# Fill products and new orders of begin and end in a kernel of four conditioned residual layers

## The chip, the cores and the metric

One core of a Trainium2 chip. The metric is the time of one execution on the device, in microseconds (us), of this core. Each kernel is run several times; the median counts. The profile is of one execution of its own: its span runs from the first to the last instruction, and some time lies around it.

## The reference

Inputs are x, 128 entries of 64 rows of 256 numbers, and per entry a vector of 128, one of 64 and one of 32. Four layers follow, each added to its input:

```python
x = x + L0(x)   # U = mu @ W_dec + b_dec, (257, 30) per entry; weight = U @ V; out = x @ weight + bias
x = x + L1(x)   # styles = mu @ affine.T; (x * styles) @ weight.T * dcoefs + bias, clipped to +-256
x = x + L2(x)   # relu(x @ (down * dg + db)) @ (up * ug + ub) + x, gains and offsets from mu
x = x + L3(x)   # below
# L3: h = ln(ln(x, pw[id]), cp[id]); t = ln(x, tm[id]); s = ln(x, ms[id])
#     m, n, r = x + mlp_ln(memory), x + mlp_ln(noise), x + mlp_ln(resource)
#     out = mlp_ln(concat(w0 h, w1 t, w2 m, w3 n, w4 r, w5 s)), w = softmax(aw)
```

Here `mlp_ln` is two matrix products with a silu between them and a layer norm behind. What hangs on the entry alone (U, styles, dcoefs, the gains of L2, the three small nets) is computed once ahead of the blocks.

## The kernel before, in words

The 8192 rows are cut into 16 blocks of 512 (8 entries each). A block goes through some sixty stages on four engines. TensorE (PE) has 17 stages per block, ScalarE (ACT) 17, VectorE (DVE) 19, GpSimd (POOL) 9; SyncE (SP) issues the loads and stores. Stages of one engine run in an order that is written out by hand: `run_slots` (L81) goes through the list `begin`, then ten times through `order` (the loop, for all blocks in turn: a pair (stage, lag) runs for the block that many behind), then through `end`. A pair (stage, n) in `begin` and `end` is that stage for block n. Each engine runs its list strictly in order; a stage waits on semaphores for what it reads and for the tiles that it overwrites.

The data of a block: `pe_t` and `pe_x1` (L0, L919, L935) give x1; POOL's `g_style` (L1516) makes xm; `pe_l1` (L948) and DVE's `v_l1mul`, `v_l1min`, `v_x2add` (L1352, L1361, L1367) make x2; `pe_dn` (L962), `v_dnmul`, `v_dnadd`, `act_relu`, and `pe_up` (L976) make x3. The weights of `pe_up` are made by POOL's `g_wup` (two products of tensors, L1565 and L1567) from a tile `ugub` that is loaded per block. `pe_x3r` (L988) turns x3, `v_xstat` takes the statistics, `g_rootx` (L1523 to L1531) the inverse root, `act_xnorm` (L1209) xhat; `g_gather` (L1507) fetches four tiles of table rows by indirect DMAs, `g_hmul` and `g_hadd` (L1546, L1551) make h, `v_hstat`, `g_rooth`, `act_hnorm`, `v_hprod` finish it. `g_res` (L1577) makes x3be, which only the last step of a block reads. `pe_xht`, `pe_hht` (L994) are transposes, `pe_tm` (L1008), `pe_ms`, `pe_cp` look up gains by onehot products, `pe_shift` (L1074) and `pe_w1_x3`, `pe_w1_tm`, `pe_w1_ms`, `pe_w1_h` (L902 to L904) sum the first product of the last MLP, `pe_w2` (L1132 and L902 to L904) is the second; `act_ysquare`, `v_ygain`, `g_rooty`, `v_ynorm` are the last layer norm. In the last three blocks (`fine`) the silu and the second product are cut in halves.

Ahead of the blocks stands the setup. The decoder: `load_dec` brings W_dec, 16 groups of up to four matrices are copied into another order by `act_turn` (L696, 11 groups) and `v_turn` (L587, 5 groups), multiplied by `pe_dec` (L487) and taken from PSUM by `v_decode` (L595) into six banks used in turn. W_dec's place in memory is used again: `load_w2n`, `load_w1` and `load_rown` (L456, L465, L460) wait for the last product of the decoder (`m_dec` of 16). Three nets run through `pe_hid`, `act_hid`, `pe_mo`, `v_mostat`, `g_moroot`, `v_monorm`, `pe_mot`, `act_mot`, `pe_row`; `pe_cls` and `v_classes` make the class rows. `act_ubwrite` (L701) issues three writes of the bias rows, `act_ug` (L727, L729) writes the table that `load_up` reads. `v_dcrcp` and `g_dcoef` make dcoefs, which `v_l1mul` 0 waits for. `g_w2low`, `g_w1xlow`, `g_w1tlow`, `g_w1mlow` (L832 to L846) make the low halves of the last MLP's weights.

`pe_warm` (L531 to L537) runs products of a tile of ones that nobody reads, into a PSUM bank that is free at the time. In the kernel before it has four places with 13, 13, 7 and 13 products; each place waits for one semaphore, given in its table, and for five of POOL's memsets. The tile of ones is set in `g_init` (L796), behind seven DMA issues of POOL.

## Time and profile before

| | us |
|---|---|
| three runs | 521.61, 525.68, 526.17 |
| median | 525.68 |
| profiled execution | 521.21 |
| its span | 519.4 |
| one block of the loop on PE | 27.8 |
| first block of the loop starts on PE | 96.7 |

The rows are read so: in a timeline, the first number is the start in us, the second how long the instruction or the merged group (xcount) took, then engine, line, operation, the tile written and the tiles read. What stands in brackets is the idle time of the engine ahead of it and what ended it. PE's weight loads are a row of their own (PEld). One f32 product is two records.

### The profile page before, as it was taken

The page shows a single profiled execution, that of the slowest core. Times are in us where ns is not written, and L with a number is a line of the kernel's source. Part 1 is how long each engine was busy: PE and PEld are TensorE (multiplying, and loading weights), DVE is VectorE, ACT ScalarE, POOL GpSimd, SP SyncE. Part 2 cuts the span into 40 slices and gives each one's busy share as a digit, 9 for nine tenths or more (in the row PEclk, how much of TensorE's full clock was granted, in tenths as well). Part 3 has the DMA queues.
Part 4 walks back from the last instruction along what each step waited for, and adds up shares of the span by engine and source line. Part 5 has one row for each costly group of instructions (what it writes and reads, how often), then busy time and mean ns, then how long its engine had stood idle before and what let it go on. Part 6 is the DMA issues. An engine that isn't in the chain of part 4 may idle for free.

```text
span 519.4 us, 9425 instructions
## 1 busy us (share of the span) xinstructions
PE 486.3 (94%) x3198; PEld 354.2 (68%) x3198; DVE 405.8 (78%) x696; ACT 336.3 (65%) x638; POOL 391.0 (75%) x367
## 2 busy tenths in 40 slices
PE   2987887999999999999999999999999999998993
PEld 2953644767677776768686867677776768687682
DVE  2958876868788788888787878788787888886863
ACT  4573667456767676766777776767676767656832
POOL 6468799889878879697978787788779793787321
PEclk9999999999999999999999999999999999999997
DMA  8887705625252352608080716253442613104102
GB/s 299 247 304 208 203 20 124 163 73 135 83 127 81 77 171 56 191 24 223 0 229 17 205 43 173 74 136 112 106 142 63 175 47 90 49 21 145 40 2 81
DMA packets 34989, 61.78 MB, mean 119 GB/s; under 512 B 5017, under 2 KB 17413, under 8 KB 34580
## 3 DMA queue, kind: packets, MB, share of 16 engines
q1 hardware_dynamic: 28756, 43.98, 30.2%
q0 software_dynamic: 5344, 16.87, 11.3%
q10 hardware_dynamic: 864, 0.61, 0.4%
q8 instruction: 14, 0.23, 0.2%
q14 instruction: 11, 0.09, 0.1%
HBM read 52.58 MB, written 8.87 MB: 118 GB/s over the span
## 4 chain that ended last, share of the span: by engine, by line
PE 79%; POOL 6%; DVE 5%; DMA 4%; issue 3%; ACT 2%; SPq 0%; DVEq 0%; POOLq 0%; ACTq 0%
PE ps_c L902 11%; PE ps_c L904 11%; PE ps_c L903 10%; PE ps_d L948 9%; PE ps_d L962 5%; PE ps_a L976 5%; PE ps_b L902 3%; PE ps_b L903 3%; PE ps_b L904 3%; PE ps_b L935 2%; PE ps_a L988 2%; DMA set_wdec<-in_nets_rows 2%; PE ps_a L994 2%; PE ps_b L994 2%; DMA set_wdec<-in_W_dec 1%
## 5 line engine op out<-in xcount | busy, mean ns | idle before, releaser
L1507 POOL DMA_INDIRECT pw_rows<-in_pw,gidx x64 | 65.0, 1016 | 17.9 <-issue 17.4
L948 PE MATMUL ps_d<-xm_t,l_w 128*128 128x512 f32 x128 | 59.0, 603 | 2.2 <-POOL xm_t L1516 2.2
L1209 ACT ACTIVATE h<-h,nb_h,rstd_h 128x256 f32<-128x256 f32 x64 | 33.3, 591 | 33.1 <-POOL nb_h L1531 33.0
L1240 ACT ACTIVATE tm_t_h<-ps_a 128x1024 fp32r<-128x1024 f32 x16 | 16.4, 1026 | 45.6 <-DVE ps_a L1413 45.6
L1516 POOL TENSOR_TENSOR xm_t<-x_t,style 128x1024 f32<-128x1024 f32 x16 | 30.5, 1905 | 20.2 <-DVE x_t L1345 20.1
L948 PEld LDWEIGHTS ps_d<-xm_t,l_w 128*128 128x128 f32 x128 | 23.1, 190 | 26.8 <-issue 24.2
L1546 POOL TENSOR_TENSOR h<-xhat,pw_rows 128x1024 f32<-128x1024 f32 x16 | 38.0, 2378 | 4.1 <-ACT xhat L1209 4.1
L1565 POOL TENSOR_TENSOR w_up<-up_rep,ugub 128x1024 f32<-128x1024 f32 x16 | 38.0, 2372 | 2.2 <-issue 2.0
L1551 POOL TENSOR_TENSOR h<-h,pw_rows 128x1024 f32<-128x1024 f32 x16 | 38.3, 2394 | 1.3
L1567 POOL TENSOR_TENSOR w_up<-w_up,ugub 128x1024 f32<-128x1024 f32 x16 | 38.1, 2382 | 1.3
L902 PE MATMUL ps_b<-w_h,act_t_l 128*128 128x256 f32 x128 | 37.7, 294 | 0.4 <-DVE act_t_l L1450 0.4
L1577 POOL TENSOR_TENSOR x3be<-x,ln_gb 128x1024 f32<-128x1024 f32 x16 | 37.8, 2364 | 0.0
L1352 DVE TENSOR_TENSOR ps_d<-ps_d,dcoef 128x1024 f32<-128x1024 f32 x16 | 19.7, 1232 | 21.6 <-PE ps_d L948 21.6
L903 PE MATMUL ps_b<-w_l,act_t_h 128*128 128x256 f32 x128 | 36.1, 282 | 0.0
L904 PE MATMUL ps_b<-w_h,act_t_h 128*128 128x256 f32 x128 | 36.0, 281 | 0.0
L1209 ACT ACTIVATE xhat<-ps_a,nb_x,rstd_x 128x256 f32<-128x256 f32 x64 | 31.0, 564 | 6.7 <-POOL nb_x L1531 6.7
L962 PE MATMUL ps_d<-x_t,down_w 128*64 128x256 f32 x256 | 31.2, 385 | 3.0 <-DVE x_t L1367 3.0
L976 PEld LDWEIGHTS ps_a<-act_dn,w_up 128*128 128x128 f32 x256 | 30.5, 191 | 4.9 <-issue 2.6
L976 PE MATMUL ps_a<-act_dn,w_up 128*128 128x128 f32 x256 | 31.6, 277 | 2.2 <-ACT act_dn L1188 1.2
L1590 POOL TENSOR_TENSOR ve_y<-y_var,eps 128x4 f32<-128x4 f32 x15 | 3.0, 202 | 40.2 <-ACT y_sq L1320 40.2
L1418 DVE TENSOR_TENSOR ps_d<-ps_d,xh_t 128x1024 f32<-128x1024 f32 x16 | 19.7, 1231 | 17.4 <-PE ps_d L1031 17.4
L1320 ACT ACTIVATE y_sq<-ps_b 128x256 bf16<-128x256 f32 x64 | 23.7, 380 | 14.8 <-PE ps_b L904 14.8
(251 smaller groups left out, 1551.2 us busy)
## 6 DMA issues: line engine op xcount, KB each, us to landing
ugub<-ugub_scratch SPq DMA_DIRECT2D x32, 512.0 KB, 6.8
x_t<-in_x_t SPq DMA_DIRECT2D x16, 512.0 KB, 5.7
out<-y_out SPq DMA_DIRECT2D x15, 512.0 KB, 7.3
set_wdec<-in_W_dec SPq DMA_DIRECT2D x2, 1920.0 KB, 9.6
set_wdec<-in_int_W SPq DMA_DIRECT2D x1, 1536.0 KB, 9.8
set_wdec<-in_nets_rows SPq DMA_DIRECT2D x1, 1152.0 KB, 12.2
pw_rows<-in_pw,gidx POOLq DMA_INDIRECT x64, 3.7
set_wdec<-in_nets_W SPq DMA_DIRECT2D x1, 768.0 KB, 4.8
```

Source lines behind the costliest of these rows:

```text
L902: eng.matmul(out, wl, ah, start=first, stop=False)
L903: eng.matmul(out, wh, al, start=False, stop=False)
L904: return eng.matmul(out, wh, ah, start=False, stop=last)
L948: m = eng.matmul(ps_l1[:, o, :], l1_w[:, k, o * P:(o + 1) * P], xm_t[:, k, :], start=k == 0, stop=k == KB - 1)
L962: m = eng.matmul(ps_dn[e * HID:(e + 1) * HID, part * CT * S:(part + 1) * CT * S], down_w[:, k, part * HID:(part + 1) * HID], x[:, k, e], s ...
L976: m = eng.matmul(ps_up[:, k, j * P:(j + 1) * P], w_up[:, j, k * P:(k + 1) * P], act_dn[:, j, :, :], start=True, stop=True)
L1209: m = eng.activation(out[:, j, :], src[:, j, :], ACT.Identity, bias=nb[k][:, j:j + 1], scale=rstd[k][:, j:j + 1])
L1507: eng.indirect_dma_start(pw_rows[c.ring][:, j, :], None, t["pw"], bass.IndirectOffsetOnAxis(ap=gidx[c.ring][:, j:j + 1], axis=0)).then_inc ...
L1546: eng.tensor_tensor(h1[:, :, :], xhat[:, :, :], pw_rows[c.ring][:, :, 0:D], ALU.mult).then_inc(g_h1m, 1)
L1551: eng.tensor_tensor(h1[:, :, :], h1[:, :, :], pw_rows[c.ring][:, :, D:2 * D], ALU.add).then_inc(g_h1, 1)
L1565: eng.tensor_tensor(w_up[:, :, :], q, ugub[:, :, 0:D], ALU.mult).then_inc(g_upm, 1)
L1567: eng.tensor_tensor(w_up[:, :, :], w_up[:, :, :], ugub[:, :, D:2 * D], ALU.add).then_inc(g_up, 1)
```

## The change

The loop's orders and SP's list are unchanged. POOL sets the tile of ones first of all (`g_ones`), and `pe_warm` waits for that alone. It has seven places in its table `WARM` (semaphore, value, bank, half, count): 27 products ahead of the decoder, 6 ahead of `pe_mo`, 23 ahead of `pe_dn` 0, 12 ahead of `pe_dn` 1, 4 behind it, 9 ahead of `pe_t` 3 and 11 ahead of `pe_hht` 0. That is 92 products where 46 were. `begin` and `end` of all four engines get new orders. The stages themselves and their durations are the same. The lists of ScalarE, VectorE and POOL are shown as they are after the change; those of before stand above.

```diff
@@ -409,6 +409,9 @@
         pads = (ubias_p[:, :], act_dn[:, :, :, :], onehot[0][:, :], onehot[1][:, :], shift[0][:, :], shift[1][:, :], gain_tab[:, 2 * D:3 * D],)
 
 
+        WARM = ((z_pool, 1, ps_b, 0, 27), (c_ug, 1, ps_d, 0, 6), (v_dca, 1, ps_a, 0, 23), (v_x1, 2, ps_b, 0, 4),
+                (v_row, 1, ps_c, 0, 12), (v_cls, 1, ps_c, 1, 9), (v_row, 1, ps_c, 0, 11))
+
         def load_front(eng, c):
             eng.dma_start(mu, t["cond_side"][:, 0:B]).then_inc(d_front, 16)
             eng.dma_start(wtail[:, :], t["W_dec"][:, D * RK:(D + 1) * RK]).then_inc(d_front, 16)
@@ -529,12 +532,11 @@
             m.then_inc(m_mo, 1)
 
         def pe_warm(eng, c):
-            s, v, out, count = ((c_ug, 1, ps_d[:, 0, :], 13), (v_dca, 1, ps_a[:, 0, :], 13),
-                                (v_x1, 2, ps_b[:, 0, :], 7), (v_x1, 2, ps_b[:, 0, :], 13))[c.n]
-            eng.wait_ge(z_pool, 5)
+            s, v, ps, k, count = WARM[c.n]
+            eng.wait_ge(z_pool, 1)
             eng.wait_ge(s, v)
             for _ in range(count):
-                eng.matmul(out, ones[:, :], ones[:, :].unsqueeze(1).broadcast_to([P, CH // P, P]), start=True, stop=True)
+                eng.matmul(ps[:, k, :], ones[:, :], ones[:, :].unsqueeze(1).broadcast_to([P, CH // P, P]), start=True, stop=True)
 
         def pe_mot(eng, c):
             eng.wait_ge(d_id, 16)
@@ -778,6 +780,9 @@
                 m = eng.activation(b2_row[lo:lo + PIECES, :], b2_row[0:PIECES, :], ACT.Copy)
             m.then_inc(c_shift, 1)
 
+
+        def g_ones(eng, c):
+            eng.memset(ones[:, :], 1.0).then_inc(z_pool, 1)
 
         def g_init(eng, c):
             ncp = PIECES * NCP
@@ -793,7 +798,6 @@
             eng.memset(mhalf[:, :], -0.5).then_inc(z_pool, 1)
             eng.memset(mone[:, :], -1.0).then_inc(z_pool, 1)
             eng.memset(eps4[:, :], EPS).then_inc(z_pool, 1)
-            eng.memset(ones[:, :], 1.0).then_inc(z_pool, 1)
             eng.memset(down_w[:, :, HID:P], 1.0).then_inc(z_pool, 1)
             eng.wait_ge(d_gain, 64)
             eng.wait_ge(z_pool, 5)
@@ -1615,30 +1619,31 @@
         @block.tensor
         def _(eng):
             run_slots(eng,
-                      begin=[(pe_dec, 0), (pe_tail, 0), (pe_dec, 1), (pe_dec, 2), (pe_dec, 3), (pe_dec, 4),
-                             (pe_dec, 5), (pe_dec, 6), (pe_dec, 7), (pe_dec, 8), (pe_dec, 9), (pe_dec, 10),
-                             (pe_dec, 11), (pe_style, 0), (pe_dec, 12), (pe_dec, 13), (pe_dec, 14), (pe_dec, 15),
-                             (pe_ug, 0), (pe_t, 0), (pe_dc, 0), (pe_hid, 0), (pe_x1, 0), (pe_warm, 0), (pe_mo, 0),
-                             (pe_l1, 0), (pe_t, 1), (pe_warm, 1), (pe_dn, 0), (pe_mot, 0), (pe_up, 0), (pe_x1, 1),
-                             (pe_cls, 0), (pe_x3r, 0), (pe_row, 0), (pe_l1, 1), (pe_xht, 0), (pe_t, 2),
-                             (pe_warm, 2), (pe_dn, 1), (pe_warm, 3), (pe_up, 1), (pe_x1, 2), (pe_x3r, 1),
-                             (pe_cp, 0), (pe_t, 3), (pe_l1, 2), (pe_shift, 0), (pe_tm, 0), (pe_hht, 0), (pe_dn, 2),
-                             (pe_w1_x3, 0), (pe_ms, 0)],
+                      begin=[(pe_warm, 0), (pe_tail, 0), (pe_dec, 0), (pe_dec, 1), (pe_dec, 2), (pe_dec, 3),
+                             (pe_dec, 4), (pe_dec, 5), (pe_dec, 6), (pe_dec, 7), (pe_dec, 8), (pe_dec, 9),
+                             (pe_dec, 10), (pe_dec, 11), (pe_style, 0), (pe_dec, 12), (pe_dec, 13),
+                             (pe_dec, 14), (pe_dec, 15), (pe_ug, 0), (pe_t, 0), (pe_dc, 0), (pe_x1, 0),
+                             (pe_hid, 0), (pe_warm, 1), (pe_mo, 0), (pe_l1, 0), (pe_warm, 2), (pe_dn, 0),
+                             (pe_t, 1), (pe_mot, 0), (pe_x1, 1), (pe_up, 0), (pe_cls, 0), (pe_t, 2),
+                             (pe_x3r, 0), (pe_row, 0),  (pe_l1, 1), (pe_xht, 0), (pe_warm, 4),
+                             (pe_dn, 1), (pe_warm, 3), (pe_up, 1), (pe_cp, 0), (pe_x1, 2), (pe_x3r, 1),
+                             (pe_warm, 5), (pe_t, 3), (pe_l1, 2), (pe_warm, 6), (pe_hht, 0), (pe_tm, 0),
+                             (pe_dn, 2), (pe_shift, 0), (pe_w1_x3, 0), (pe_ms, 0)],
                       order=[(pe_xht, 5), (pe_w1_tm, 6), (pe_up, 4), (pe_w1_ms, 6), (pe_cp, 5), (pe_x1, 3),
                              (pe_w1_h, 6), (pe_x3r, 4), (pe_t, 2), (pe_l1, 3), (pe_hht, 5), (pe_shift, 5),
                              (pe_w1_x3, 5), (pe_tm, 5), (pe_dn, 3), (pe_w2, 6), (pe_ms, 5)],
                       end=[(pe_xht, 11), (pe_w1_tm, 10), (pe_up, 12), (pe_w1_ms, 10), (pe_cp, 11), (pe_x1, 13),
-                           (pe_w1_h, 10), (pe_x3r, 12), (pe_t, 14), (pe_l1, 13), (pe_shift, 11), (pe_hht, 11),
+                           (pe_w1_h, 10), (pe_t, 14), (pe_x3r, 12), (pe_l1, 13), (pe_shift, 11), (pe_hht, 11),
                            (pe_w1_x3, 11), (pe_dn, 13), (pe_tm, 11), (pe_w2, 10), (pe_ms, 11), (pe_xht, 12),
-                           (pe_w1_tm, 11), (pe_up, 13), (pe_w1_ms, 11), (pe_x1, 14), (pe_cp, 12), (pe_w1_h, 11),
-                           (pe_x3r, 13), (pe_t, 15), (pe_l1, 14), (pe_shift, 12), (pe_hht, 12), (pe_w1_x3, 12),
+                           (pe_w1_tm, 11), (pe_up, 13), (pe_w1_ms, 11), (pe_x1, 14), (pe_x3r, 13), (pe_cp, 12),
+                           (pe_w1_h, 11), (pe_t, 15), (pe_l1, 14), (pe_shift, 12), (pe_hht, 12), (pe_w1_x3, 12),
                            (pe_tm, 12), (pe_dn, 14), (pe_w2, 11), (pe_ms, 12), (pe_xht, 13), (pe_w1_tm, 12),
-                           (pe_up, 14), (pe_w1_ms, 12), (pe_cp, 13), (pe_x1, 15), (pe_w1_h, 12), (pe_x3r, 14),
-                           (pe_l1, 15), (pe_hht, 13), (pe_shift, 13), (pe_w1_x3, 13), (pe_tm, 13), (pe_dn, 15),
+                           (pe_up, 14), (pe_cp, 13), (pe_w1_ms, 12), (pe_x1, 15), (pe_w1_h, 12), (pe_x3r, 14),
+                           (pe_l1, 15), (pe_shift, 13), (pe_hht, 13), (pe_w1_x3, 13), (pe_tm, 13), (pe_dn, 15),
                            (pe_w2, 12), (pe_ms, 13), (pe_xht, 14), (pe_w1_tm, 13), (pe_up, 15), (pe_w1_ms, 13),
-                           (pe_cp, 14), (pe_w1_h, 13), (pe_x3r, 15), (pe_ms, 14), (pe_hht, 14),
-                           (pe_shift, 14), (pe_w1_x3, 14), (pe_tm, 14), (pe_w2, 13), (pe_w1_ms, 14),
-                           (pe_w1_tm, 14), (pe_w1_h, 14), (pe_xht, 15), (pe_cp, 15), (pe_tm, 15), (pe_shift, 15),
+                           (pe_cp, 14), (pe_w1_h, 13), (pe_x3r, 15), (pe_ms, 14), (pe_shift, 14), (pe_hht, 14),
+                           (pe_w1_x3, 14), (pe_tm, 14), (pe_w2, 13), (pe_w1_ms, 14), (pe_w1_tm, 14),
+                           (pe_cp, 15), (pe_w1_h, 14), (pe_xht, 15), (pe_shift, 15), (pe_tm, 15),
                            (pe_w1_x3, 15), (pe_hht, 15), (pe_ms, 15), (pe_w1_tm, 15), (pe_w2, 14),
                            (pe_w1_ms, 15), (pe_w1_h, 15), (pe_w2, 15)],
                       fill=6)
@@ -1647,32 +1652,33 @@
         def _(eng):
...
+                             (act_ubwrite, 0), (act_turn, 7), (act_turn, 9), (act_turn, 10), (act_turn, 12),
+                             (act_style, 0), (act_gidx, 0), (act_turn, 13), (act_turn, 15), (act_dg, 0),
+                             (act_w2high, 0), (act_u, 0), (act_th1, 0), (act_gidx, 1), (act_th2, 0),
+                             (act_exp, 0), (act_ug, 0), (act_hid, 0), (act_sqrt, 0), (act_u, 1),
+                             (act_w1scale, 0), (act_w1high, 0), (act_th1, 1), (act_gidx, 2), (act_th2, 1),
+                             (act_relu, 0), (act_mot, 0), (act_u, 2), (act_u, 3), (act_th1, 2), (act_x3, 0),
+                             (act_onehot, 0), (act_xnorm, 0), (act_x3h, 0), (act_th2, 2),
+                             (act_xht, 0), (act_relu, 1), (act_rowwrite, 0), (act_hnorm, 0), (act_onehot, 1), (act_th1, 3),
+                             (act_x3, 1), (act_u, 4), (act_xnorm, 1), (act_shift, 0), (act_hh, 0), (act_th2, 3),
+                             (act_gidx, 3), (act_tmh, 0), (act_relu, 2), (act_msh, 0), (act_xht, 1),
+                             (act_x3h, 1), (act_hnorm, 1), (act_silu, 0), (act_th1, 4), (act_th2, 4),
+                             (act_silh, 0), (act_x3, 2), (act_gidx, 4), (act_xnorm, 2), (act_hh, 1),
+                             (act_tmh, 1), (act_onehot, 2), (act_ysquare, 0), (act_relu, 3), (act_xht, 2),
+                             (act_msh, 1), (act_x3h, 2)],
                       order=[(act_u, 1), (act_hnorm, 4), (act_silu, 5), (act_gidx, 1), (act_silh, 5),
...
+                      end=[(act_u, 15), (act_hnorm, 12), (act_silu, 11), (act_silh, 11), (act_x3, 13),
+                           (act_th1, 15), (act_xnorm, 13), (act_hh, 12), (act_tmh, 12), (act_gidx, 15),
+                           (act_relu, 14), (act_th2, 15), (act_x3h, 13), (act_ysquare, 11), (act_msh, 12),
+                           (act_xht, 13), (act_onehot, 13), (act_hnorm, 13), (act_silu, 12), (act_silh, 12),
+                           (act_x3, 14), (act_hh, 13), (act_xnorm, 14), (act_tmh, 13), (act_x3h, 14),
+                           (act_onehot, 14), (act_ysquare, 12), (act_relu, 15), (act_xht, 14), (act_msh, 13),
+                           (act_hnorm, 14), (act_sil0, 13), (act_onehot, 15), (act_sil1, 13), (act_x3, 15),
+                           (act_hh, 14), (act_xnorm, 15), (act_msh, 14), (act_x3h, 15), (act_tmh, 14),
+                           (act_ysquare, 13), (act_sil0, 14), (act_sil1, 14), (act_xht, 15), (act_hnorm, 15),
...
@@ -1680,58 +1686,59 @@
         @block.vector
         def _(eng):
...
+                      begin=[(v_turn, 2), (v_pads, 0), (v_turn, 5), (v_decode, 0), (v_ubias, 0), (v_decode, 1),
...
+                             (v_decode, 6), (v_turn, 11), (v_w2centre, 0), (v_turn, 14), (v_decode, 7),
+                             (v_decode, 8), (v_decode, 9), (v_decode, 10), (v_decode, 11), (v_decode, 12),
+                             (v_decode, 13), (v_stylesq, 0), (v_decode, 14), (v_decode, 15), (v_awmax, 0),
+                             (v_l1sq, 0), (v_dceps, 0), (v_softmax, 0), (v_x1add, 0), (v_dcrcp, 0),
+                             (v_mostat, 0), (v_w1sum, 0), (v_l1mul, 0), (v_l1min, 0), (v_x2add, 0),
+                             (v_monorm, 0), (v_dnmul, 0), (v_dnadd, 0), (v_gains, 0), (v_x3sum, 0),
+                             (v_x1add, 1), (v_classes, 0), (v_xstat, 0), (v_rows, 0), (v_l1mul, 1),
+                             (v_l1min, 1), (v_x2add, 1), (v_dnmul, 1), (v_dnadd, 1), (v_hstat, 0), (v_x3low, 0),
+                             (v_x3sum, 1), (v_x1add, 2), (v_hprod, 0), (v_xstat, 1), (v_l1mul, 2), (v_l1min, 2),
+                             (v_x2add, 2), (v_tmprod, 0), (v_hlow, 0), (v_dnmul, 2), (v_dnadd, 2), (v_tmlow, 0),
+                             (v_msprod, 0), (v_mslow, 0), (v_hstat, 1), (v_x3low, 1), (v_x3sum, 2)],
+                      order=[(v_x1add, 3), (v_hprod, 5), (v_xstat, 4), (v_sillow, 6), (v_l1mul, 3),
+                             (v_l1min, 3), (v_x2add, 3), (v_hlow, 5), (v_tmprod, 5), (v_dnmul, 3), (v_dnadd, 3),
+                             (v_tmlow, 5), (v_msprod, 5), (v_ygain, 6), (v_mslow, 5), (v_hstat, 4),
+                             (v_ynorm, 6), (v_x3low, 4), (v_x3sum, 3)],
                       end=[(v_x1add, 13), (v_hprod, 11), (v_xstat, 12), (v_sillow, 10), (v_l1mul, 13),
...
+                           (v_tmlow, 12), (v_msprod, 12), (v_ygain, 11), (v_x3low, 13), (v_mslow, 12),
+                           (v_hstat, 13), (v_ynorm, 11), (v_x3sum, 14), (v_x1add, 15), (v_hprod, 13),
...
+                           (v_hstat, 14), (v_msprod, 13), (v_mslow, 13), (v_x3low, 14), (v_ygain, 12),
+                           (v_ynorm, 12), (v_hprod, 14), (v_x3sum, 15), (v_sil0, 13), (v_xstat, 15),
+                           (v_msprod, 14), (v_sil1, 13), (v_hlow, 14), (v_mslow, 14), (v_tmprod, 14),
+                           (v_tmlow, 14), (v_x3low, 15), (v_ygain, 13), (v_ynorm, 13), (v_hstat, 15),
+                           (v_sil0, 14), (v_sil1, 14), (v_tmprod, 15), (v_hprod, 15), (v_tmlow, 15),
+                           (v_msprod, 15), (v_hlow, 15), (v_mslow, 15), (v_ygain, 14), (v_ynorm, 14),
+                           (v_sil0, 15), (v_sil1, 15), (v_ygain, 15), (v_ynorm, 15)],
...
         @block.gpsimd
         def _(eng):
...
+                      begin=[(g_ones, 0), (g_init, 0), (g_b2rows, 0), (g_w2low, 0), (g_style, 0), (g_gather, 0),
+                             (g_dcoef, 0), (g_moroot, 0), (g_w1tlow, 0), (g_wup, 0), (g_w1xlow, 0),
+                             (g_gather, 1), (g_style, 1), (g_rootx, 0), (g_wup, 1), (g_hmul, 0), (g_hadd, 0),
+                             (g_rooth, 0), (g_w1mlow, 0), (g_style, 2), (g_res, 0), (g_rootx, 1), (g_gather, 2),
+                             (g_hmul, 1), (g_hadd, 1), (g_wup, 2), (g_rooth, 1), (g_style, 3), (g_res, 1),
+                             (g_rootx, 2), (g_gather, 3)],
                       order=[(g_wup, 3), (g_hmul, 4), (g_hadd, 4), (g_rooty, 6), (g_gather, 2), (g_rooth, 4),
...
+                      end=[(g_wup, 13), (g_hmul, 12), (g_hadd, 12), (g_rooty, 10), (g_gather, 14),
+                           (g_rooth, 12), (g_style, 14), (g_res, 12), (g_rootx, 13), (g_wup, 14), (g_hmul, 13),
+                           (g_hadd, 13), (g_gather, 15), (g_rooty, 11), (g_rooth, 13), (g_style, 15),
+                           (g_res, 13), (g_rootx, 14), (g_hmul, 14), (g_hadd, 14), (g_wup, 15), (g_rooty, 12),
+                           (g_rooth, 14), (g_res, 14), (g_rootx, 15), (g_hmul, 15), (g_rooty, 13), (g_hadd, 15),
+                           (g_rooth, 15), (g_rooty, 14), (g_res, 15), (g_rooty, 15)],
...
```

## Rows read from the trace of the kernel before

**Rows 1.** Page: busy by engine; granted TensorE clock in 40 slices
```profile
PE 486.3 (94%) x3198; PEld 354.2 (68%) x3198; DVE 405.8 (78%) x696; ACT 336.3 (65%) x638; POOL 391.0 (75%) x367
...
PEclk9999999999999999999999999999999999999997
```

**Rows 2.** Stages: PE, PEld, DVE, ACT, POOL busy (xcount), PEclk, DMA share, GB/s
```profile
9.47:13.44 3.97, 3.97 (x19) 3.97 (x19) 1.17 (x7) 3.97 (x4) 3.05 (x4) 1.00 1.02 409
...
26.70:60.00 33.30, 26.98 (x194) 15.28 (x194) 24.41 (x42) 21.67 (x41) 26.59 (x25) 1.00 0.85 245
60.00:96.70 36.70, 31.29 (x221) 18.53 (x221) 27.69 (x55) 22.89 (x43) 34.07 (x27) 1.00 0.39 103
96.70:374.90 278.20, 277.96 (x1852) 202.84 (x1851) 227.74 (x375) 188.41 (x359) 226.43 (x202) 1.00 0.41 112
374.90:474.60 99.70, 99.55 (x619) 73.65 (x617) 84.08 (x144) 67.72 (x129) 74.66 (x71) 1.00 0.34 99
474.60:519.40 44.80, 33.31 (x191) 26.85 (x190) 25.76 (x41) 21.90 (x50) 13.75 (x15) 0.93 0.11 37
```

**Rows 3.** PE's timeline: start, us, line, operation, tiles, xcount, idle before it
```profile
9.47 2.04 PE L487 MATMUL ps_a<-set_mu,set_w_rt 128*128 128x128 f32 x8 [9.47 <-ACT set_w_rt L696]
...
15.96 1.95 PE L487 MATMUL ps_d<-set_mu,set_w_rt 128*128 128x128 f32 x16
...
25.14 1.58 PE L487 MATMUL ps_c<-set_mu,set_w_rt 128*128 128x128 f32 x12
...
44.59 2.98 PE L537 MATMUL ps_a<-ones 128*128 128x512 bf16 x13
...
87.27 0.59 PE L1074 MATMUL ps_c<-onehot,shift 128*128 128x512 bf16 x2
...
91.47 1.95 PE L962 MATMUL ps_d<-x_t,down_w 128*64 128x256 f32 x16 [1.19 <-DVE x_t L1367]
...
100.41 2.02 PE L976 MATMUL ps_a<-act_dn,w_up 128*128 128x128 f32 x16
```

**Rows 4.** ACT's timeline, first 19 us
```profile
8.15 5.41 ACT L696 ACTIVATE set_w_rt<-set_wdec 128x512 f32<-128x512 f32 x5 [6.13 <-DMA set_wdec<-in_W_dec]
13.30 2.02 ACTq L701 DMA_DIRECT2D ub_scratch<-set_ubias_p  x3
```

**Rows 5.** The chain that ended last, in order of time, 28 to 119 us
```profile
28.22 12.19 DMA set_wdec<-in_nets_rows
...
115.61 1.05 POOL rstd_x L1526
...
119.34 1.88 PE ps_d L962 x16
```

**Rows 6.** DVE's timeline: the end of block 0's x2
```profile
47.37 1.22 DVE L1367 SCALAR_TENSOR_TENSOR x_t<-ps_d,x_t 128x1024 f32<-128x1024 f32 x1
```

**Rows 7.** POOL's timeline, 64 to 102 us
```profile
64.75 2.35 POOL L1577 TENSOR_TENSOR x3be<-x,ln_gb 128x1024 f32<-128x1024 f32 x1
...
79.24 1.27 POOL L836 TENSOR_TENSOR w_l<-set_w1x,w_h 128x512 fp32r<-128x512 f32 x1
...
81.70 1.91 POOL L1516 TENSOR_TENSOR xm_t<-x_t,style 128x1024 f32<-128x1024 f32 x1
...
85.40 1.01 POOL L1526 TENSOR_TENSOR rstd_x<-ve_x,mhalf 128x4 f32<-128x4 f32 x1
...
86.64 2.34 POOL L1565 TENSOR_TENSOR w_up<-up_rep,ugub 128x1024 f32<-128x1024 f32 x1
...
91.37 2.38 POOL L1546 TENSOR_TENSOR h<-xhat,pw_rows 128x1024 f32<-128x1024 f32 x1
...
96.40 1.04 POOL L1507 DMA_INDIRECT pw_rows<-in_pw,gidx  x1 [0.17 <-POOL h L1551]
```

**Rows 8.** PE's timeline near the end: two waits
```profile
476.21 0.39 PE L1008 MATMUL ps_a<-onehot,gain_tab 24*128 24x512 bf16 x2 [1.50 <-ACT xhat L1209]
...
490.40 0.39 PE L1008 MATMUL ps_a<-onehot,gain_tab 24*128 24x512 bf16 x2 [1.19 <-ACT xh_t L1230]
```

58 lines of the change are left out of this document (removed).

## The prediction

> **What bounds the kernel now.** I read the page first: TensorE (PE) is busy 94% of the span, the granted clock is full until the last slice [rows 1]. Then the stages [rows 2]: from 96.7 us, where the loop's first block begins on PE, to 474.6 us, PE is busy 277.96 of 278.20 us and 99.55 of 99.70 us. The loop is PE's own work, and its text is unchanged: ten blocks at 27.8 us each, nothing to win or lose there. What the change can move is the 96.7 us ahead of it and the 44.8 us behind 474.6. In the first, PE does nothing before 9.47 us, is idle 33.30 - 26.98 = 6.3 us between 26.7 and 60 and 36.70 - 31.29 = 5.4 us between 60 and 96.7 [rows 2], and part of its busy time is fill (46 products; 13 of them take 2.98 us, so 0.229 us each [rows 3]). Idle time of PE is worth something only if the operation that ends it comes earlier, so I went through each engine's order of time and the chain that ended last [rows 5]: the decoder; a 12.19 us load of the nets' rows, which waits for the decoder's last product; VectorE; then, from 60 to 92 us, POOL, which is busy 34.07 of 36.70 us [rows 2]; and at 115.6 us POOL once more, before PE takes over for good [rows 5]. So the begin is set by the decoder's end and by POOL's list.
>
> **27 products ahead of the decoder.** They need only the ones tile, now POOL's first instruction. The decoder's first 8 records take 2.04 us where 16 later ones take 1.95 [rows 3]: 0.255 against 0.122 us, the lower and the upper of TensorE's levels (1.2 and 2.4 GHz) after 9.5 us without work. All of the stretch up to 13.44 us holds 19 records in 3.97 us [rows 2], so about 4 us run at the lower level. The fill takes that over: 27 x 0.229 = 6.2 us if all at the upper level, 12.4 us at the lower; with 4 us at the lower (9 products) and 18 x 0.229 = 4.1 us it is 8.1 us, from about 1 us on, done at 9.1 us. The first turned weights exist at about 9.3 us (8.15 + 5.41 / 5 [rows 4]), so I cost it at nothing; all at the lower level it would end at 13.4 and cost 4 us. Saved on PE: 16 x (0.255 - 0.122) = 2.1 us. Not all of it arrives. ScalarE turns a group in 1.08 us, stops for the three bias writes until 15.3 us [rows 4], and its new order puts the style activation, which waits for PE's style products behind group 11, ahead of turns 13 and 15 (1.08 + 0.54 us); these are then late, where before PE was. VectorE's zeroing of the pads now runs behind its first turn instead of in the wait for the weights; PE's first groups cover it. I take 1.0 us for the decoder's end, 26.7 -> 25.7 us, between 0 and 2.1.
>
> The Trainium skill, TensorE: Matmul & The Clock Gate, Part 1, has the array slow by default and freed by activity, which the row bears out; it also puts the ramp below 1% of a typical span and warns not to fit a count. By that this part is small, as in my sum (2.1 of 519 us).
>
> **To the end of block 0's x2.** The nets' rows, W1 and W2 loads start with the decoder's end, so 1.0 us earlier. On the other branch the dcoef chain moves behind gather 0 on POOL, four gathers of about 1.25 us from start to start (one is 1.04 [rows 7]), 5.0 us, but x1 0 goes ahead of the reciprocal and of the nets' first layer, so that style 0 and gather 0 begin some 3 us earlier. Both branches meet at l1mul 0. x2 0 ends at 47.37 + 1.22 = 48.6 us now [rows 6]; I take 47.6, bounds 46.5 and 50.6 (all 5 us of gather in the way, 3 given back). The 6 + 23 products that stand here are 1.4 and 5.3 us; the 23 start when l1 0 ends, about 42.3, and end at 47.6, just when x2 is there. That is tight: each us that l1 0 is late goes straight into dn 0, which queues behind the fill. The write of ugub moves 3 us later behind the softmax's exp, and with it SP's queue (load_up 0, x 2, ids 1); w_up 0 is made from 48.3 on, so this is covered.
>
> **To style 2.** Two of POOL's half-size products (w1xlow, w2low), which stand ahead of style 2 (79.24 to 81.70, 2.46 us [rows 7]), go forward into holes; x3be 0 (2.35 us) goes behind style 2. Against it stand w_up 1 moved ahead of h 0 (h 0 is then ready no sooner, and rooth 0 waits about 2 us for its statistics), w1mlow (1.3 us) ahead of style 2, and VectorE's classes ahead of xstat 0 (2.3 us on the path of rootx 0). Following the four engines' new orders with the old durations, I get style 2 at 80.3 us instead of 81.70: 1.4 us of 2.46. Bounds: 79.2 (all) and 82.5 (none, and x1 2 late by the fill). PE then does l1 2, the 11 fills (2.5 us) inside the wait for x2 2, and dn 2 at 90.5 instead of 91.47 [rows 3]. But the shift products, which lay in an idle stretch at 87.27, now stand behind dn 2, in the dense part: 0.45 us. The loop's first block starts on PE 0.5 us earlier.
>
> **The new late comer.** w_up 2 was made at 86.64, ahead of h 1 and gather 2 [rows 7]. Now it is last of the row: style 2 (1.9) + x3be 0 (2.35) + rootx 1 (1.7: 85.40 to 86.64 and two small ones) + gather 2 (5.0) + h 1 (91.37 to 96.40, 5.03) + w_up 2 (86.64 to 91.37, 4.73) = 20.7 us. From 80.3 this is 101.0 us. up 2 stood at 100.41 on PE with no wait [rows 3], and PE would now reach it at 99.9. So PE stands 1.1 us, and the block runs 0.6 us behind the old one. In return rootx 2 comes ahead of gather 3 and leaves the chain (115.61 [rows 5]), which gave PE a last wait of a quarter us: -0.2.
>
> **The end.** Two waits are left there: 1.50 us before the tm products, for xhat 15, and 1.19 us for xh_t 15 [rows 8]. The new list puts nothing new between x3r 15 and tm 14, so the first stays, and ScalarE has onehot 15 and hh 14 ahead of xnorm 15: +0.1 us. In the second, cp goes from ahead of the wait to ahead of w1_h 14 and shift 15 fills 0.2 us of it: 0. hadd 15 now waits behind rooty 13 for some 2.5 us; its cover up to hht 15 is about as long, and it costs up to 1.5 us if onehot's move doesn't bring the squares forward. I take +0.1, between -0.8 and +1.5.
>
> **Sum,** against the profiled execution (span 519.4, time 521.2, so 1.8 us around it): +0.6 - 0.2 + 0.1 = +0.5 us, span 519.9, time 521.7 us. The runs shown are 521.61, 525.68 and 526.17: the profiled execution is like the fastest of them and 4.5 us below their median. So my time is 0.8% below the median and the same as the profiled execution. About 1% is what a measurement of this kernel can tell from no change.
>
> **Rivals.** (a) *The begin comes through.* If the decoder gives 2.1 us and POOL's two products all of 2.46, style 2 starts at 78.8 to 79.2, w_up 2 is done at 99.7, and PE keeps 1.5 to 2.5 us: 519 us. For it: w_up 2 is my only late comer, and 1.1 us decides. Against: ScalarE's turns and VectorE's classes.
> (b) *The spread stays.* Something that no single trace shows costs two of three runs 4.5 us. If it is the clock falling in the holes of the begin (idle 6.3 and 5.4 us [rows 2]) or a longer slow stretch of the decoder (each further 4 us at 0.255 us a record costs 2), the fills end it and the forecast stands as a median. If it is anything else (loads, launch), the new kernel has it too: 521.7 + 4 = 525.7 us, no change. The same page and part of the Trainium skill call the ramp's place variable from run to run, which would favour the fills; one trace can't show it.
> (c) *Slower: the fill in front of dn 0.* If l1 0 ends later than 42.3 us by d, dn 0 starts at 47.6 + d whatever x2 does. With gather 0's 5 us in the way d is about 3, style 2 starts 3 us later than reckoned (83.3), w_up 2 is done at 104.0 and up 2 runs 3.6 us late; with 1.5 us at hadd 15: 526.5 us; with the first fill at the lower level throughout (4 us) 530.5. It decides from d = 0.5 on. For it: POOL's order; against: PE's mo and l1 products lie there with little in front.
>
> **How the numbers follow.** Forecast 0.43 (520.4 to 523.5), (a) 0.30, (b) 0.17, (c) 0.10. Range: 518.3 (under half of (a) lies below 518.8) to 526.0. Faster by over 1% means below 520.4: (a) 0.30 and the lower edge of the forecast 0.04; slower by over 1%, above 530.9, only the tail of (c): 0.03.
>
> **What would show it.** Right: PE's fill from about 1 us, ending before 9.5; the decoder's first records at 0.12 us each and its last at 25.7; x2 0 at 47.6; style 2 at 80.3; a wait of about 1 us at up 2 for w_up 2; the loop at 27.8 us a block; two waits of 1.5 and 1.2 us near the end. Wrong: dn 0 starting straight behind the 23 fills with x2 long done; style 2 later than 82; a wait of PE inside the loop; the clock falling anywhere before the last slice.

## The result and the profile after

The changed kernel takes 530.88 us in the median of four runs (530.81 to 533.24), the kernel before 523.64 beside it (520.94 to 526.17): a ratio of 1.018, 95% interval 1.014 to 1.022. That is 9.2 us above the forecast of 521.7 and outside the range. The profiled execution has a span of 531.4 us against 519.4. It is the one of 533.24 us, 2.3 to 2.4 us slower than the other three, while the profiled one of the kernel before is among its fastest: the 12.0 us between the two profiles are more than the 7.2 us between the medians.

The page of the changed kernel, TensorE's (PE's) busy time and its granted clock, beside [rows 1]:

```profile
PE 502.6 (95%) x3215; PEld 360.7 (68%) x3244; DVE 408.9 (77%) x696; ACT 336.4 (63%) x639; POOL 391.6 (74%) x367
...
PEclk9979899999989999999999999999999999999998
```

PE is busy 16.3 us longer, with the same products of the computation and 92 filling ones instead of 46. The clock, which in the kernel before fell in the last slice alone, is below full in three more places. Five stages of the changed kernel, cut at the same instructions as in the kernel before (the decoder's end, x3r 0, the start of `pe_xht` in blocks 1, 3 and 12, the last instruction; `pe_xht` is the first stage of each round of the loop, and xht 1 the first round); columns as in [rows 2]:

```profile
26.07:63.19 37.12, 31.67 (x229) 18.38 (x229) 27.08 (x42) 20.43 (x39) 28.38 (x25) 0.91 0.77 219
63.19:100.72 37.53, 34.76 (x208) 21.18 (x204) 26.96 (x54) 23.25 (x43) 29.73 (x26) 0.95 0.37 107
100.72:162.92 62.20, 57.56 (x367) 41.16 (x370) 43.19 (x71) 35.18 (x64) 49.74 (x41) 0.97 0.39 97
162.92:412.96 250.04, 248.80 (x1648) 182.16 (x1665) 207.73 (x343) 173.45 (x334) 201.26 (x180) 1.00 0.40 111
412.96:531.40 118.44, 106.26 (x617) 80.04 (x623) 87.00 (x146) 69.52 (x141) 65.02 (x67) 0.98 0.25 73
```

and the same of the kernel before (the fourth, 250.01 us, left out):

```profile
26.70:59.86 33.16, 26.84 (x194) 15.14 (x193) 24.41 (x42) 21.67 (x41) 26.45 (x25) 1.00 0.85 245
59.86:96.68 36.82, 31.41 (x222) 18.65 (x222) 27.69 (x55) 22.86 (x43) 34.19 (x27) 1.00 0.40 104
96.68:152.63 55.95, 55.71 (x371) 40.56 (x370) 43.22 (x71) 34.33 (x63) 47.29 (x42) 1.00 0.42 107
...
402.64:519.40 116.76, 105.27 (x623) 80.51 (x623) 86.70 (x146) 70.29 (x141) 66.06 (x66) 0.97 0.24 72
```

The stage lengths differ by +4.0, +0.7, +6.3, 0.0 and +1.7 us; the decoder's end is 0.6 earlier. From the loop's third round on, nothing changed. But its first two rounds, with an unchanged list, lost 6.3 us: they work off what the begin left behind. What was lost lies in blocks 0 and 1, in these two rounds, and behind 413 us.

PE's own timeline shows where (columns as in [rows 3]):

```profile
1.08 8.10 PE L539 MATMUL ps_b<-ones 128*128 128x512 bf16 x27 [1.08 <-POOL ones L785]
...
9.57 2.14 PE L490 MATMUL ps_a<-set_mu,set_w_rt 128*128 128x128 f32 x16
...
44.34 5.13 PE L539 MATMUL ps_a<-ones 128*128 128x512 bf16 x23
49.39 1.95 PE L966 MATMUL ps_d<-x_t,down_w 128*64 128x256 f32 x16
...
62.45 0.22 PE L917 MATMUL ps_b<-entry_oh,ub_ch 6*128 6x128 bf16 x1 [2.33 <-DVE x_t L1349]
...
106.18 2.05 PE L980 MATMUL ps_a<-act_dn,w_up 128*128 128x128 f32 x16 [1.65 <-POOL w_up L1571]
...
147.63 1.80 PE L952 MATMUL ps_d<-xm_t,l_w 128*128 128x512 f32 x3 [2.63 <-DVE h L1432]
...
485.72 0.39 PE L1078 MATMUL ps_c<-onehot,shift 128*128 128x512 bf16 x1 [1.13 <-DVE act_t_l L1460]
...
487.85 0.39 PE L1012 MATMUL ps_a<-onehot,gain_tab 24*128 24x512 bf16 x2 [0.35 <-ACT xhat L1213]
```

The first fill is done at 9.18 and the decoder's records start at 0.13 us each, where [rows 3] had 0.255. Then dn 0 at 49.39 follows the 23 fills without a hole (48.74 before), t 2 waits 2.33 us for x1add 1, up 2 waits 1.65 for w_up 2, l1 4 waits 2.63 at 147.63, and the wait of 1.50 at xhat [rows 8] is now 0.35, with a new one of 1.13 ahead of it (1.48 together).

VectorE's and GpSimd's (POOL's) timelines at 50 to 60 us, changed kernel:

```profile
53.17 2.14 DVE L669 TENSOR_TENSOR later<-cls_const,mone 24x1 f32<-24x1 f32 x1
...
55.51 1.43 DVE L390 TENSOR_SCALAR set_tab<-set_tab_p,cls_const 24x768 f32<-24x768 bf16 x1
```

```profile
50.51 2.37 POOL L1569 TENSOR_TENSOR w_up<-up_rep,ugub 128x1024 f32<-128x1024 f32 x1 [1.03 <-DMA ugub<-ugub_scratch]
52.95 2.34 POOL L1571 TENSOR_TENSOR w_up<-w_up,ugub 128x1024 f32<-128x1024 f32 x1
55.26 1.27 POOL L840 TENSOR_TENSOR w_l<-set_w1x,w_h 128x512 fp32r<-128x512 f32 x1
```

In the kernel before these gain operations took 0.19 and 0.61 us at 52.98 and 53.39; now the first ends when POOL's second half of w_up 0 ends, and the one of 1.43 us ends 0.4 us behind the low part of W1. The gains take 6.6 us instead of 3.9, and w_up 0 stands at 50.51 instead of 46.72. x1add 1 ends at 62.4 instead of 59.5.

POOL between blocks 2 and 4, changed kernel:

```profile
114.12 1.90 POOL L1520 TENSOR_TENSOR xm_t<-x_t,style 128x1024 f32<-128x1024 f32 x1 [4.98 <-DVE x_t L1349]
...
120.67 1.05 POOL L1511 DMA_INDIRECT pw_rows<-in_pw,gidx  x1 [0.64 <-issue]
...
125.49 2.38 POOL L1569 TENSOR_TENSOR w_up<-up_rep,ugub 128x1024 f32<-128x1024 f32 x1
```

It is idle for 4.98 us ahead of style 3, and only then gathers the rows of block 3, ahead of w_up 3. w_up 3 starts 8.5 us later than in the kernel before (117.02), where PE had been 4.0 us late at xht 1; what stands behind it on POOL is late with it, until l1 4 waits at 147.6 for the tile that block 2's h product on VectorE still holds.

### The profile page after: what moved, and what is told of

It is laid out like the page before. It is cut to its first block, busy times and chain, and to the rows that moved or that the text cites. A ratio compares the mean times of both kernels' runs of the same rounds, so it can differ in the third digit from the quotient of the medians.

```text
span 531.4 us, 9492 instructions
## 1 busy us (share of the span) xinstructions
PE 502.6 (95%) x3215; PEld 360.7 (68%) x3244; DVE 408.9 (77%) x696; ACT 336.4 (63%) x639; POOL 391.6 (74%) x367
## 4 chain that ended last, share of the span: by engine, by line
PE 71%; POOL 9%; DVE 8%; issue 5%; DMA 4%; ACT 2%; SPq 1%; DVEq 0%; POOLq 0%; ACTq 0%
PE ps_c L906 10%; PE ps_c L908 9%; PE ps_c L907 9%; PE ps_d L952 8%; PE ps_d L966 4%; PE ps_a L980 4%; PE ps_b L906 3%; PE ps_b L907 2%; PE ps_b L908 2%; PE ps_a L992 2%; DMA set_wdec<-in_W_dec 2%; PE ps_b L939 2%; POOL pw_rows L1511 2%; PE ps_b L998 2%; PE ps_a L998 2%
## 5 line engine op out<-in xcount | busy, mean ns | idle before, releaser
L952 PE MATMUL ps_d<-xm_t,l_w 128*128 128x512 f32 x128 | 60.5, 616 | 2.6 <-DVE h L1432 2.6
```

Of the source, the lines that this page charges most:

```text
L952: m = eng.matmul(ps_l1[:, o, :], l1_w[:, k, o * P:(o + 1) * P], xm_t[:, k, :], start=k == 0, stop=k == KB - 1)
```

## The experiments

Each run has its own runs of the kernel before beside it; "xht n" is the start of `pe_xht` in block n. Medians in us, ratio to the kernel before with its 95% interval; xht 0, 3, 12 and the span are of the profiled execution. The kernel before's median beside the changed kernel was 523.64, beside the others 521.7 to 522.9. Times of runs that were not made together are set against each other below; the kernel before's own median moved by up to 1.9 us between such sets, so that a difference of 1 us is not clear of noise.

| run | median | ratio | xht 0 | xht 3 | xht 12 | span |
|---|---|---|---|---|---|---|
| before | 521.7 to 522.9 | 1 | 66.98 | 152.63 | 402.64 | 519.4 |
| changed | 530.88 | 1.018 (1.014-1.022) | 71.82 | 162.92 | 412.96 | 531.4 |
| e1 | 526.41 | 1.011 (1.004-1.017) | 68.07 | 153.72 | 403.67 | 522.3 |
| e2 | 529.59 | 1.015 (1.013-1.018) | 71.76 | 161.19 | 411.24 | 528.0 |
| e18 | 525.12 | 1.004 (1.000-1.007) | 70.52 | 156.19 | 406.24 | 525.9 |
| e4 | 527.09 | 1.011 (1.008-1.014) | 69.58 | 156.06 | 406.18 | 525.0 |
| e6 | 529.52 | 1.014 (1.008-1.019) | 70.64 | 159.27 | 409.42 | 527.7 |
| e9 | 528.99 | 1.013 (1.009-1.017) | 72.21 | 161.36 | 411.54 | 529.8 |
| e13 | 526.24 | 1.007 (1.004-1.010) | 70.97 | 156.66 | 406.64 | 525.0 |
| e3 | 524.95 | 1.005 (1.002-1.007) | 67.94 | 153.59 | 403.60 | 520.4 |
| e11 | 527.81 | 1.011 (1.007-1.015) | 73.58 | 159.24 | 409.25 | 526.0 |
| e5 | 531.71 | 1.019 (1.013-1.024) | 72.46 | 161.37 | 411.32 | 529.9 |
| e7 | 528.33 | 1.012 (1.007-1.018) | 69.48 | 158.36 | 408.44 | 526.7 |
| e10 | 531.51 | 1.018 (1.014-1.023) | 70.65 | 161.21 | 411.16 | 529.5 |
| e14 | 527.75 | 1.008 (1.004-1.012) | 73.58 | 159.13 | 409.19 | 525.9 |
| e16 | 524.90 | 1.004 (1.001-1.007) | 70.45 | 156.00 | 406.14 | 522.9 |
| e8 | 524.46 | 1.004 (1.002-1.006) | 70.47 | 156.14 | 406.23 | 523.0 |
| e12 | 521.47 | 0.999 (0.995-1.002) | 66.18 | 155.12 | 405.25 | 522.0 |
| e15 | 520.28 | 0.996 (0.993-0.999) | 66.94 | 152.62 | 402.89 | 519.7 |
| e17 | 522.84 | 1.000 (0.997-1.002) | 67.26 | 152.92 | 403.27 | 521.6 |

How much one execution's begin can tell must be said first. The kernel before, e1 and e18 have the same begin, and xht 0 came at 66.98, 68.07 and 70.52; the changed kernel, e2, e4, e6 and e13 have the same lists up to there, and it came at 71.82, 71.76, 69.58, 70.64 and 70.97. A difference at xht 0 of up to 3.5 us between two profiles can thus be one of executions. The steps behind it repeat better: from xht 3 to xht 12 it is 249.9 to 250.4 us in all twenty kernels.

**The end.** e1 is the kernel before with the new end lists, e2 the changed kernel with the old ones.

> The kernel before with only the new ends of the four engines; begin and fill as before. Theory 1 (the loss of 12.0 us in span is made in the begin and in the loop's first blocks; xht 12, the first of the end to show it, is 10.3 us late and the last instruction 12.0): the ends alone cost 1.7 us, so about 521 to 523 in span against 519.4. Theory 2 (the ends are harmless and the last 1.7 us come from the phase in which POOL enters them): within 0.5 us of before.

> The changed kernel with the ends of before. Theory 1: 1.7 us under the changed kernel, span about 529.7 or, against the three quicker executions of it (529.0), 527.3. Theory 2: nothing gained, 529 to 531.

From xht 12 to the last instruction it is 116.8 us in the kernel before and in e2, 118.4 in the changed kernel and 118.6 in e1: the ends cost 1.7 to 1.9 us, and theory 1 holds. The median of e2 is 1.3 below the changed kernel's; e1's, 4.4 above the kernel before, comes from four runs that lie between 523.3 and 529.5 and says less. I first took ScalarE's onehot 15 (1.97 us), now between the two halves of silu 13, for the cause:

```diff
 # e18 = e1 with, on ScalarE's end
-(act_hnorm, 14), (act_sil0, 13), (act_onehot, 15), (act_sil1, 13),
+(act_hnorm, 14), (act_sil0, 13), (act_sil1, 13), ... (act_tmh, 14), (act_onehot, 15),
```

> The kernel before with the new ends of all engines, except that ScalarE does onehot 15 behind tmh 14 and no longer between the two halves of silu 13. With onehot there the first run of this study had waits of 1.14 and 0.34 us for the second half of silu 13 and xhat, then 1.51 at xh_t, and cost 1.9 us in the trace. Theory 1 (onehot 15 is the cost): the wait of 1.14 us goes, the end takes 1.5 to 2 us less than with the new ends, total within 0.7 us of the kernel before. Rival (the order of TensorE, shift 13 and hht 13 exchanged, or hadd 15 behind rooty 13 costs): the end stays 1 us or more longer than in the kernel before, total 1 to 2 us above it.

That theory fell. VectorE and PE of e18:

```profile
477.52 1.21 DVE L1418 TENSOR_TENSOR ps_d<-ps_d,xh_t 128x1024 f32<-128x1024 f32 x1
478.64 0.68 DVE L1456 TENSOR_TENSOR act_t_l<-ps_c,act_t_h 128x512 fp32r<-128x512 f32 x1
```

```profile
479.37 0.39 PE L1074 MATMUL ps_c<-onehot,shift 128*128 128x512 bf16 x1 [1.14 <-DVE act_t_l L1456]
```

ScalarE has its second half ready at 475.7, but VectorE does msprod 14 (1.21 us) first and then the low part of that half, which PE waits for: the 1.14 us wait is unchanged, and the end is 119.7 us long. In the old list msprod 14 stood behind it. But this wait is not the cost either. With the 0.34 us at xhat behind it (0.35 in the changed kernel) it is as long as the one wait of 1.50 us that the old end has there. The loss stands ahead of it: x3r 15, in the kernel before and in e1, is

```profile
468.97 1.04 PE L988 MATMUL ps_a<-ident,x_t 128*128 128x128 f32 x8
```

```profile
471.44 1.09 PE L988 MATMUL ps_a<-ident,x_t 128*128 128x128 f32 x8
```

which is 66.3 and 67.8 us behind xht 12 (67.6 in the changed kernel), at the full clock and with no wait of PE above 0.3 us. So 1.3 to 1.4 of the 1.7 to 1.9 us are lost there, by the new order of what stands ahead of x3r 15; most of the rest is the wait at xh_t, 1.51 us for 1.19. Which of the exchanges costs this, no run took apart; the rival of e18, the order of TensorE's list, is open. e18's span is longer mainly because its xht 0 came late (70.52).

**Blocks 2 to 5.** All three start from the changed kernel:

```diff
 # e4
-(g_style, 3), (g_res, 1), (g_rootx, 2), (g_gather, 3)
+(g_gather, 3), (g_style, 3), (g_res, 1), (g_rootx, 2)
 # e6
-(g_rootx, 1), (g_gather, 2), (g_hmul, 1), (g_hadd, 1), (g_wup, 2),
+(g_rootx, 1), (g_wup, 2), (g_gather, 2), (g_hmul, 1), (g_hadd, 1),
```

e9 has both of these, the gain operations of e7 and the old ends.

> The changed kernel with one stage moved on POOL: gather 3 ahead of style 3, into the 5 us that POOL stands idle there. Theory 1 (the 4.7 us that the block from 130 to 163 us loses, 2.6 us of waiting for h 2 and a stretch at half clock, come from POOL's gather 3 lying behind that idle stretch): the wait at 147 us and the fall of the clock go, 4 to 5 us less, span 524 to 527. Rival (style 3 or rootx 2 are then late and take its place): within 1 us of the changed kernel.

> The changed kernel with w_up 2 back in its old place on GpSimd, behind the first root of block 1 and ahead of gather 2 and h 1. Theory 1 (up 2 waits 1.65 us for w_up 2 and passes that on whole): the wait goes, xht 2 near 129 instead of 130.5, total 1.0 to 1.6 us less, near 529.2. Rival (h 1 and gather 2, now 4.8 us later, take its place as the late comer): the wait is replaced by one for h 1 or a gathered row of the same size and the total stays within 0.5 us of 530.5.

> The changed kernel with four things of its lists taken back or moved: gather 3 ahead of style 3, w_up 2 behind the first root of block 1 (old place), the gain operations in VectorE's idle time behind x1add 0, and the old ends on all engines. Theory 1 (the loss is the sum of places that don't cover each other): their single effects, taken against the changed kernel's 530.9, add to 3.8 + 1.4 + 2.6 + 1.3 = 9.1 us, total near 521.8 to 523, level with the kernel before; in the trace xht 0 near 69.5, steps of 28.4, 28.0, 28.4, then 27.8, xht 12 near 404. Rival (the single effects overlap, the late begin is passed on through GpSimd's queue in another place as soon as one wait is gone): a new wait over 1 us shows in blocks 1 to 3, total 525 or more.

e4: the step from xht 2 to xht 3 is 28.39 instead of 32.46 us, the wait at 147 is 0.26, and the median falls by 3.8. The largest single item is thus gather 3 behind style 3. Its size varies: in e2, e5 and e7, which have the same order, this step was 30.8 us. e6: the wait at up 2 goes, the step xht 1 to 2 is 27.96 instead of 29.74; the median falls by 1.4. e9 is a miss: 529.0 where 521.8 to 523 was expected. PE and POOL of e9:

```profile
117.66 2.38 PE L952 MATMUL ps_d<-xm_t,l_w 128*128 128x512 f32 x3 [2.78 <-POOL xm_t L1520]
```

```profile
100.57 2.40 POOL L1550 TENSOR_TENSOR h<-xhat,pw_rows 128x1024 f32<-128x1024 f32 x1
...
110.78 1.04 POOL L1511 DMA_INDIRECT pw_rows<-in_pw,gidx  x1 [0.64 <-issue]
...
115.60 1.91 POOL L1520 TENSOR_TENSOR xm_t<-x_t,style 128x1024 f32<-128x1024 f32 x1
```

With w_up 2 early and gather 2 still ahead of h 1, h 1 begins at 100.57, its root and gather 3 come late, and style 3, now behind gather 3, starts at 115.60, so l1 3 waits 2.78 us. Both single moves were right alone and wrong together. e13 puts POOL's old order back behind rootx 1, all else as changed (x3be 0 stays behind style 2):

```diff
 # e13
+(g_style, 2), (g_res, 0), (g_rootx, 1), (g_wup, 2), (g_hmul, 1), (g_hadd, 1), (g_gather, 2),
+(g_rooth, 1), (g_res, 1), (g_style, 3), (g_gather, 3), (g_rootx, 2)
```

> The changed kernel with GpSimd's order of the kernel before from style 2 on (w_up 2 ahead of h 1, gather 2 behind h 1, gather 3 ahead of the root of block 2); all else as changed. Theory 1 (what blocks 2 to 5 lose is this order as a whole; the run with four things back failed only because gather 2 was left ahead of h 1): no PE wait over 1.3 us between 100 and 170, the steps of xht are 28.4, 28.1, 27.8, xht 4 near 184 instead of 190.7 with xht 0 at 71.8, total 5.5 us less than the changed kernel, near 525.3. Rival (the late begin finds another wait in blocks 1 to 3 in any order): a wait over 1.5 us and total 527 or more.

```profile
99.49 1.04 POOL L1511 DMA_INDIRECT pw_rows<-in_pw,gidx  x1 [0.16 <-POOL h L1555]
...
111.08 1.91 POOL L1520 TENSOR_TENSOR xm_t<-x_t,style 128x1024 f32<-128x1024 f32 x1 [0.87 <-DVE x_t L1349]
113.15 1.04 POOL L1511 DMA_INDIRECT pw_rows<-in_pw,gidx  x1 [0.16 <-issue]
```

Gather 2 fills the time in which the root of h 1 would wait, gather 3 that of the root of x 2, and POOL is idle 0.87 us ahead of style 3 instead of 4.98. From xht 0 to xht 3 it is 85.69 us (before 85.65, changed 91.10, e2 with the same order as the changed kernel 89.43); the median falls by 4.6. All that blocks 1 to 3 lost is this order.

**The begin.** e3 is the kernel before with the first fill alone, e11 the kernel before with gather 0 ahead of the demodulation's root (g_dcoef).

> The kernel before with the tile of ones set first and 27 products ahead of the decoder; nothing else. Theory 1 (the first fill works: the decoder's end 1 to 2 us earlier, and the fall of the clock in the changed kernel has another cause): span 517.5 to 519, and the runs of before that take 4.5 us more than the others lose their spread. Rival (a fill of 8 us moves the point at which the clock falls, or costs as much as it gives): span 519.4 or more, and the granted clock falls somewhere before 60 us.

> The kernel before with one move: gather 0 on GpSimd ahead of the demodulation's root, as far as that goes as in the change. Theory 1 (the transfers of 28 to 50 us are bound by their sum; the gathered rows, asked for at 32 instead of 40, push the nets' rows and the u-gains behind them): the nets' rows land later than 40.9, w_up 0 waits for its u-gains or starts later than 46.7, the root and with it l1 0 come 1.4 us later (gather ends near 36.8), xht 0 near 68.4 instead of 67.0, total 1 to 1.5 us more than the kernel before. Rival (GpSimd had 3.6 us of idle time there, and its queue is 5 us shorter afterwards): style 0 at most 1 us later, w_up 0 at 42 to 44, gather 1 ahead of the gains, total level or up to 1 us less.

```profile
41.87 0.97 DVE L630 TENSOR_TENSOR ps_c<-ps_c,set_wdec 128x768 f32<-128x768 f32 x1 [7.10 <-DMA set_wdec<-in_nets_rows]
```

```profile
49.70 3.00 PE L965 MATMUL ps_d<-x_t,down_w 128*64 128x256 f32 x16 [3.76 <-DVE x_t L1370]
```

In e3 the decoder and PE's mo and l1 products end 1.6 us earlier, and dn 0 comes 1.0 us later than in the kernel before: VectorE waits 7.10 us for the nets' rows until 41.87, with l1mul 0 queued behind. The rows' load starts 2.1 us earlier and ends some 1.0 later; SyncE's load of the u-gains, issued at 34.82 instead of 36.24, runs beside it. Where that load is issued at about 40, as in the changed kernel, e4, e6 and e13, VectorE starts on the rows at 40.1 to 41.1; where at 34.7 to 36.2, in e1, e3, e5, e14 and e18, at 41.8 to 43.0 (the kernel before and e11, issued at 36.2 and 36.3, had 40.9 and 41.0). That transfers beside each other are the reason is a guess: no run changed it alone, and the same begin with the load issued at the same time had VectorE start at 40.92 in the kernel before and at 42.85 in e18. In the changed kernel VectorE's start at 41.10 waited for PE, not for the rows. In the median e3 is 0.5% slower than the kernel before (interval 1.002 to 1.007).

e11 cost 6 us, where 1 to 1.5 was expected, and by another way:

```profile
38.24 0.74 POOL L806 TENSOR_TENSOR set_dm<-set_dm 128x256 f32<-128x256 f32 x1
...
41.05 1.90 POOL L1516 TENSOR_TENSOR xm_t<-x_t,style 128x1024 f32<-128x1024 f32 x1
...
48.40 2.35 POOL L1565 TENSOR_TENSOR w_up<-up_rep,ugub 128x1024 f32<-128x1024 f32 x1 [2.88 <-DMA ugub<-ugub_scratch]
```

```profile
43.09 6.47 PE L948 MATMUL ps_d<-xm_t,l_w 128*128 128x512 f32 x8 [3.80 <-POOL xm_t L1516]
```

The rows land as before. The gather does not begin until 33.30, and the root and style 0 come 2.85 us later (style 0 at 38.20 before), l1 0 waits 3.80 and runs at half the clock (6.47 instead of 3.67 us). w_up 0 then waits 2.88 us for the u-gains.

e5 puts ScalarE's u-gain write ahead of th1 0 and w_up 0 ahead of the low part of W1 in the changed kernel; e7 moves the gain operations into VectorE's idle time behind x1add 0; e10 adds 11 filling products in PE's idle times at 22 to 31 us.

> The changed kernel with two things put back: ScalarE's exp and u-gain copy (with its write to the scratch tensor) ahead of th1 0 again, and w_up 0 on GpSimd ahead of the low part of W1 again. Theory 1 (the late write, landed 40.19 instead of 36.24, holds w_up 0 until 50.5; up 0 and, through GpSimd's long tensor operation, VectorE's small gain operations come late: 2.14 and 1.43 us where they took 0.19 and 0.61): the write lands near 37, w_up 0 ends near 52, the gain operations take 3.9 us again instead of 6.6, x1add 1 ends near 59.8, xht 0 near 68.5 instead of 71.8, total 3 us less, near 527.5. Rival (the lower clock of TensorE between 32 and 40 us is what is passed on): the gains come back but dn 0 and xht 0 stay within 1 us of 49.4 and 71.8, total within 1 us of 530.5.

> The changed kernel with VectorE's gain operations moved ahead into its idle time behind x1add 0 (33 to 38 us). Theory 1 (the gain operations, 6.6 us long since GpSimd's w_up 0 stands beside them, stand between dn 0 and x1add 1, for which t 2 and x3r 0 wait): they take 3.9 us or less in the new place, x1add 1 ends near 58.5 instead of 62.4, the 2.33 us wait of t 2 goes, x3r 0 starts near 60.1, xht 0 near 68.5, total 3 us less. Rival (up 0, at 55.4 for w_up 0, sets the pace and the gains only filled the wait): x3r 0 not before 62, total within 1 us of 530.5.

> The changed kernel with 11 more of the filling products in its three idle times of TensorE between 22 and 31 us: 4 ahead of group 13 of the decoder, 3 ahead of the u-gain product, 4 ahead of x1 0. Theory 1 (these idle times are what brings the granted clock to half from 33 to 39 us, since the kernel before had no fall there with a fill of 13 at 33 and fewer idle times ahead of it): the clock stays at 1.00 from 30 to 40, hid, fill and mo take 1.5 to 2.5 us less, xht 0 near 70.5 instead of 71.8, median 0.5 to 1.3 us less than 530.9. Rival (the fall comes from elsewhere, or varies from execution to execution whatever stands there): a fall in 30 to 40 or 50 to 70 remains, median within 0.4 us of 530.9.

e5 gained nothing: the load was issued at 35.3 instead of 40.2, yet w_up 0 waited for it until 49.60, and the rows were late (42.75), so dn 0 came at 50.57. e7 gained 2.5 us in the median, near theory 1; but its xht 0, 69.48, is not 68.5, and e4, with VectorE's begin unchanged, had 69.58, so the profile does not show where the gain lies. The wait of t 2 is gone, and up 0 at 55.9, waiting 1.59 us for w_up 0, is what is late next. VectorE and POOL of e7:

```profile
33.13 2.19 DVE L390 TENSOR_SCALAR set_tab<-set_tab_p,cls_const 24x768 f32<-24x768 bf16 x1
```

```profile
33.01 1.90 POOL L1520 TENSOR_TENSOR xm_t<-x_t,style 128x1024 f32<-128x1024 f32 x1 [1.90 <-DVE x_t L1349]
```

The operation that took 0.61 us beside gathers takes 2.19 beside style 0 and ends 0.4 us after that is over. e10: no gain (531.5), near what its rival has. The clock stayed full from 30 to 40 us in its profile, and fell at 54 to 59 and from 147 on instead. The first part is no merit of the added products: e6, e7, e13 and e16 lack them, and their clock was full from 30 to 42 us as well (`pe_mo` takes 2.86 us there, against 3.95, 4.19 and 4.06 in the changed kernel, e2 and e9).

e14 is e13 with the old ends and the first part of ScalarE's and POOL's begin put back; e16 is e13 with the old ends and e7's gains.

> The same with the old ends of all engines and the begin's first part put back on three places: GpSimd's root of the demodulation ahead of style 0 and gather 0, w_up 0 and gather 1 ahead of the low part of W1; ScalarE's exp and u-gain copy ahead of th1 0 and its root ahead of the hidden layer; VectorE's reciprocal ahead of x1add 0. What stays of the change: the first fill, the new fills, TensorE's begin (x1 0 ahead of the hidden layer, dn 0 ahead of t 1, x1 1 ahead of up 0, t 2 ahead of x3r 0), the rest of VectorE's and ScalarE's begin. Theory 1 (gather 0 ahead of the root holds up style 0 or w_up 0 through GpSimd's queue, and the gains stand beside GpSimd's tensor operations): w_up 0 starts by 47, the gains take 3.9 to 4.5 us, xht 0 near 67.5, total 520.5 to 522.5, level with the kernel before. Rival (TensorE's new order of blocks 0 and 1 is what costs): xht 0 at 69.5 or later, total 524 or more.

> The changed kernel with GpSimd's old order from style 2 on (as in the pool-tail run, 526.2), the old ends of all engines and the gain operations in VectorE's idle time behind x1add 0. Theory 1 (these three places carry most of the loss, and they add once the order of GpSimd is the old one): ends 1.3 to 1.9 us and gains 1.2 to 2.6 us less than 526.2, total 522 to 523.5; in the trace xht 0 near 69.5, steps 28.4, 28.2, 27.8 to 29.0, the end steps 27.9, 26.9, 30.5. Rival (as before, what is gained at the begin is taken by another wait or a fall of the clock): 525 or more.

```profile
43.02 0.97 DVE L631 TENSOR_TENSOR ps_c<-ps_c,set_wdec 128x768 f32<-128x768 f32 x1 [7.83 <-DMA set_wdec<-in_nets_rows]
...
57.60 2.99 DVE L392 SCALAR_TENSOR_TENSOR gain_tab<-set_tab_p,cls_const,set_tab 24x768 bf16<-24x768 bf16 x1
```

```profile
50.84 1.55 PE L966 MATMUL ps_d<-x_t,down_w 128*64 128x256 f32 x6 [3.03 <-DVE x_t L1371]
```

e14 missed by over 5 us: again the early u-gain load and late rows (43.02), dn 0 at half clock (3.49 instead of 1.95), and the gains beside POOL's low part of W1 (2.99 instead of 1.01). Its figures (xht 0 at 73.58, 527.75 us) are those that its rival asked for, TensorE's new order of blocks 0 and 1; no run took that order back alone, so the rival stands. e16, 524.9, is a miss as well: 1.3 below e13, where 2.5 or more was expected, and still 2.7 above the kernel before; its loop and end have the old lengths (85.55 and 116.8 us), and what is left stands ahead of xht 0 (70.45).

**The nets' rows first.** e8 is e3 with the nets' rows loaded ahead of W1, the gains behind x1add 0, the sum of W1's parts behind dnadd 0 and style 1 ahead of the low part of W1. e12 follows it, with 17 products ahead of dn 0 for 13; e15 follows e12; e17 is e15 without the 27 products ahead of the decoder.

```diff
 # e8, SyncE
-(load_w2n, 0), (load_w1, 0), (load_rown, 0),
+(load_w2n, 0), (load_rown, 0), (load_w1, 0),
 # e12: TensorE, ScalarE
-(pe_t, 1), (pe_warm, 1), (pe_dn, 0),
+(pe_warm, 1), (pe_dn, 0), (pe_t, 1),
-(act_hid, 0), (act_w1scale, 0), (act_w2high, 0), (act_u, 1),
+(act_hid, 0), (act_u, 1), (act_w2high, 0), (act_w1scale, 0),
 # e15: fills around l1 2, entry rows ahead of the weights
-(pe_t, 3), (pe_l1, 2),
+(pe_t, 3), (pe_warm, 5), (pe_l1, 2), (pe_warm, 6),
```

> The kernel before with the first fill (as in the third run), the load of the nets' rows ahead of the load of W1 in the queue, the gain operations behind x1add 0 on VectorE, the sum of W1's parts behind dnadd 0, and style 1 ahead of the low part of W1 on GpSimd. Theory 1 (the 1.6 us that the first fill gains at the decoder were lost because VectorE waits for the nets' rows, landed at 41.9): the rows land near 34, VectorE's statistics start at 38 with the end of the mo products, x2 0 ends near 47.0 instead of 48.6, dn 0 near 47.1, xht 0 near 65.5 instead of 67.0, total 1.5 us less than the kernel before. Rival (the transfers of these 12 us are bound by their sum, 3.4 MB, and W1, 4 us later, holds ScalarE and what follows it): ScalarE's scaling of W1 moves to 41 to 45, th2 1 and the relu come late, dn 0 at 48.5 or later, total within 1 us of the kernel before.

> The kernel with the nets' rows first (first fill, rows ahead of W1, gains early, style 1 ahead of the low part of W1) and three more moves: dn 0 ahead of t 1 on TensorE, u 1 and the high part of W2 ahead of the scaling of W1 on ScalarE, 17 instead of 13 products ahead of dn 0. In the last run x2 0 was there at 46.9, 1.7 us earlier than in the kernel before, but dn 0 came at 53.3, since t 1 ahead of it waited 4.1 us for u 1, which stood behind W1's scaling on ScalarE (W1 landed 41.7). Theory 1: dn 0 at 47.0 to 47.5, up 0 at 52.5 to 53, x1add 1 ends near 57 to 58, xht 0 near 65, total 1.5 to 2 us less than the kernel before. Rival (what stands behind, th1 1 and W1's parts, is then the late comer): xht 0 at 67 or later, total level with or above the kernel before.

> The last version with the nets' rows first, with the entry rows loaded ahead of the weights (they had held t 0 for 0.85 us), and filling products ahead of l1 2 (5) and behind it (8), where TensorE had idle times of 1.35 and 2.26 us and ran at half clock from 83 to 95. Theory 1 (the begin is 0.8 us to 1.5 us ahead of the kernel before and the fall of the clock took it back): t 0 at 27.0, xht 0 near 65.3, step to xht 1 29.7 instead of 32.96, total 2 us less than the kernel before. Rival (falls of the clock strike somewhere in any execution): a fall elsewhere between 40 and 110 us, total within 1 us of the kernel before.

> The version with the nets' rows first that ran 0.4% ahead of the kernel before, without the 27 filling products ahead of the decoder. Theory 1 (the first fill brings the decoder's end 1.6 us forward, and with the rows first nothing takes that back): decoder's last product near 26.7 instead of 25.1, xht 0 near 68.0, total 1 to 1.6 us more than with the fill, 521.5 to 522. Rival (the order of the loads is the whole gain, the begin being bound by transfers that start on the decoder's end and by VectorE): total within 0.5 us of the version with the fill, 520 to 520.8.

e8 had x2 0 at 46.9, but t 1 ahead of dn 0 waited 4.1 us for u 1, and it took 524.5, 0.4% more than the kernel before where 1.5 us less was expected. e12 mended that wait; behind one of 1.35 us its l1 2 took 5.37 us for 3.67, and it came out level (1.5 to 2 us less was expected). PE of e15:

```profile
46.91 1.95 PE L965 MATMUL ps_d<-x_t,down_w 128*64 128x256 f32 x16 [0.60 <-DVE x_t L1370]
...
52.53 3.53 PE L979 MATMUL ps_a<-act_dn,w_up 128*128 128x128 f32 x16 [1.42 <-ACT act_dn L1191]
...
83.71 3.67 PE L951 MATMUL ps_d<-xm_t,l_w 128*128 128x512 f32 x8 [0.15 <-POOL xm_t L1519]
```

In e15 dn 0 stands at 46.91 (48.74 before), l1 2 takes 3.67 us again, but up 0 takes 3.53 where 2.02 is the full clock's, and x3r 0, at 59.83, is level with the kernel before (59.86). In the medians e15 is 0.4% faster than the kernel before (interval 0.993 to 0.999), the 2 us that were expected; in the two profiles nothing of it shows (xht 0 at 66.94 and 66.98, spans of 519.7 and 519.4). Without the first fill (e17) the same kernel takes 522.8, level with the kernel before, and its xht 0 is 0.3 us later than e15's. So the medians put the first fill at some 2.5 us, once the rows come first, and at a loss without (e3). The first half of that is not clear of noise: the two ratios' intervals, 0.993 to 0.999 and 0.997 to 1.002, overlap.

## Why the prediction was wrong

The two profiles part from the forecast span of 519.9 in three places: at xht 1 (4.0 us later instead of 0.5 earlier), from xht 1 to xht 3 (6.3 us longer instead of 0.9) and in the end (1.7 longer instead of 0.1).

**27 products ahead of the decoder: right.** 8.10 us for the fill (8.1 reckoned), ending at 9.18 (9.1), records at the full clock, the decoder's last product at 26.07 instead of 25.7, with the expected wait for ScalarE's turn 13 (1.07 us). One caution: the granted clock in [rows 2] reads 1.00 for the stretch from 9.47 to 13.44, so that the lower level was at work there is read from the length of the records alone.

**To the end of block 0's x2: in its bounds.** 48.77 for 47.6; dn 0 stood in the fills' queue for 0.6 us, so the fill decided as rival (c) has it, but it was worth 0.6 and not 3. It stood there because `pe_mo` ran at the lower clock: in e6 and e13, with the same lists and the full clock, dn 0 came at 48.39 and 48.43 behind a wait of 1.68 us for x2. So this effect came and went with the execution, by the clock and not by POOL's order, which (c) names. What I had left out is the nets' rows: [rows 5] show the 12.19 us load, and I moved it forward with the decoder as if its length were fixed. In e3 it was 15.2 us long, and alone the fill gave back more than it won.

**To style 2: the first step that failed, in part open.** "I get style 2 at 80.3 us", bounds 79.2 and 82.5; it came at 85.09. I added the old durations of VectorE's and POOL's operations in the new order. But GpSimd's new order brought w_up 0 (3.8 us later) and the low parts of W1 beside VectorE's gain operations, which had stood beside gathers: +2.7 us ahead of x1add 1, and t 2, put ahead of x3r 0, made PE wait 2.33 us for it. Part of this I could have read in the Trainium skill, SBUF — State Buffer, Who interferes with whom: a VectorE instruction with two inputs in SBUF contends with a GpSimd instruction that reads SBUF, and where VectorE is in a mode that takes two ports, whichever of the two begins first holds the shared ports for its whole instruction. The traces agree (0.61 against 2.19 us, 1.01 against 2.99; the additions with one operand in PSUM stayed at 1.2 us). I also wrote that w_up 0 "is made from 48.3 on, so this is covered"; it was made from 50.51 on, 1.03 us late for its u-gains, and up 0 with it. Of the 4.5 us by which xht 1 missed, no run shows how many are these: the same lists gave xht 1 at 97.95 to 100.72, the kernel before's at 96.68 to 100.22.

**The new late comer: right, and of the right size.** w_up 2 ended 21.0 us behind style 2 (20.7 reckoned) and up 2 waited 1.65 us (1.1). e6 takes the wait away.

**"rootx 2 comes ahead of gather 3 and leaves the chain: -0.2": the sign was wrong, and this is the step that failed worst.** I looked at the root alone and not at what gather 3 had been: work for POOL while PE and VectorE make x 3. Behind style 3 and the root it holds up w_up 3 and h 2, then gather 4, the root of h 2 and l1 4. Measured: 4.7 us in the trace of the changed kernel (1.7 of them l1 4 at the lower clock), 3.0 in those of e2, e5 and e7, 3.8 in e4's median, and POOL's order as a whole 4.6 (e13).

**The end: +0.1, measured +1.7 to 1.9,** outside its bound of 1.5, and mostly in a place that I did not look at: I went through what stands behind x3r 15, and 1.3 to 1.4 us are lost ahead of it, by exchanges that no run took apart. Behind it, the waits of 1.50 and 1.19 that I kept were 1.13 + 0.35 and 1.51.

**The sum.** POOL's order from style 2 on 4.6, the gains 2.5, the ends 1.3, all measured in medians, make 8.4 us; 7.2 were lost against the runs beside it, 8.0 to 9.1 against the others. But they do not add: e16, with all three away, gained 6.0, only 1.3 more than e13 alone, and is still 2.7 us above the kernel before. So the gains' 2.5 are not shown, and 2 to 3 us of the new begin stay open (TensorE's new order, the late w_up 0 and the clock are the candidates).

Of the signs of being wrong that the prediction named, three came: style 2 later than 82, a wait inside the loop that was not forecast (l1 4), and the clock falling before the last slice.

**Rival (b), the spread,** has two visible sources. The same begin ran in e18 as in the kernel before, and its chain of waits holds this piece where [rows 5] have 12.19 us:

```profile
27.87 14.47 DMA set_wdec<-in_nets_rows
```

dn 0 came at 50.66 and xht 0 at 70.52, 3.5 us later than in the kernel before. And the granted clock over the span goes with the time: the 28 executions of the kernel before that ran beside e13 to e15 range from 520.7 to 521.7 us at 0.994 to 0.997 up to 527.9 and 528.0 at 0.981 and 0.984. The profiled execution that I reckoned from was one of the good ones. The fills did not end this.

## What to carry to other kernels

When an operation moves on an engine with a full queue, reckon what it had been covering, and move gathers only together with the roots that they stood in front of: two moves that each won 1.4 and 3.8 us alone won under 2 together with two more. Old durations hold only as long as the neighbours are the same; look up, for each VectorE operation on SBUF, what GpSimd does at its new time. An earlier start gained nothing here where the next thing waited for a transfer (e3); with the load whose user comes first put ahead of the others, the medians came out 0.4% better (e15). And profile a begin more than once before you reckon from it: its length varied by 3.5 us with nothing changed.

## What was not expected of the hardware

The granted clock of PE fell to the lower level behind quite small idle times. Three stretches of the changed kernel (columns as in [rows 2]):

```profile
34.00:36.00 2.00, 2.00 (x8) 0.94 (x7) 0.00 (x0) 1.31 (x6) 1.63 (x2) 0.50 1.13 417
64.00:66.00 2.00, 2.00 (x8) 1.79 (x7) 1.57 (x5) 0.42 (x2) 0.37 (x1) 0.50 0.96 354
147.60:153.00 5.40, 5.37 (x10) 2.33 (x11) 2.75 (x9) 4.58 (x10) 4.06 (x6) 0.68 0.00 0
```

The first two are at the lower of TensorE's two levels throughout (0.50, 1.2 GHz of 2.4), the third in part. At 34 the idle times ahead were 1.07, 0.80 and 0.98 us within 9 us, at 64 one of 2.33, at 147 one of 2.63; after 2.17 us in e16 (dn 0) it did not fall, and after 0.60, 0.67 and 1.42 in e15 it did, but not after 1.16, 1.41 and 1.21 in the kernel before (48.7 to 54.2 us). All eleven profiled executions with the old ends have an idle time of 1.50 us at xhat: behind it the clock fell in two, e9 and e17, and these ends took 118.3 us for 116.8. Each fall makes the next products take up to twice as long: 1.7 us on l1 (5.37 for 3.67), 1.5 on dn or up. It struck in different places from run to run (e10), so a hole of 1 to 3 us has a price beyond its length, but not the same one each time.

VectorE's small operations in SBUF were held by GpSimd's tensor operations: one of 0.19 us took 2.14, one of 0.61 took 2.19. The hold works both ways: GpSimd's style 0 took 2.61 us beside the gain operations in e8, 1.90 in the kernel before, e7 and e11.

The load of the nets' rows (1152 KB) took 12.2 us in one (the kernel before) and 14.5 us in another execution (e18) of the same begin.
